# Extra identity products on TensorE in the waits of a Perceiver block

## The chip, the cores and the metric

One core of a Trainium2 chip runs the whole block in one launch. The metric is the device time of that launch in microseconds (us). The engines of the core run their own instruction streams and meet at semaphores: TensorE (matmul and transposition, PE in the profile, its weight loads PEld), VectorE (DVE), ScalarE (ACT), GpSimd (POOL) and SyncE (SP), which issues most of the DMAs.

## The reference, cut to what matters

Three residual steps on 512 latent tokens of 512 numbers (batch 8 times 64), in float32:

```
x = x + cross_attention(layernorm(x), ctx)   # 16 heads of 32, ctx: 8 x 1601 tokens
x = x + self_attention(layernorm(x))         # 16 heads of 64, 4 batches as WQ, WK, WV_down, WV_up
x = x + mixture(layernorm(x))                # 8 experts of width 2048, the best 2 for each token
```

In the reference, cross attention is a softmax over the 1601 context tokens of each batch entry and a projection. Self-attention uses only the diagonal of the softmax of the scores: the values are multiplied by the probability of the token with itself and go through WV_up, and the heads are averaged. The mixture computes gates by a softmax over 8 logits, keeps the two largest, and sums the two experts' outputs by them.

## The kernel before

Float32 products are made of three products of rounded halves: `hi` is the value rounded to the fp32r type and `lo` the rest, and hi times hi, hi times lo and lo times hi are summed (`three`, L155 to L157). ScalarE makes the hi half, VectorE or GpSimd the lo half. Data is transposed on TensorE, by a matmul with the 128x128 identity `ident` in transposing mode, and comes back through one of eight PSUM banks. Where a product is taken on plain float32 (the identity selections `new_outputs`, the gathering of tokens in gating), one call gives two weight loads and two matmul records in the trace.

**Prologue.** GpSimd makes `ident`. TensorE waits for it and then for the first context tiles (`raw_in0`), turns them (L729), and multiplies with the split weights `Wkv` as these arrive, one quarter k at a time (L752).

**Cross attention.** The loop over seven batch entries and two chunks of the context interleaves, by hand, scores, transposes of the probabilities and output products with the next chunk's keys and values. The last unit (entry 7, chunk 1) has no next chunk: step i does `turn_probs(i)` (L810), `scores(i+1)` (L799), `beside(i)` and `outputs(i)` (L822). The outputs wait for the lo half of the turned probabilities `PT` from VectorE (L635, L639). `tensor_beside` puts the output selection of the last batch entry and the first parts of the projection between these. Bank 6 holds the result of the first selection until ScalarE has copied it (`o7_in`).

**Seam.** `tensor_seam` finishes the projection (L1204 to L1206) into banks 6, 1, 3 and 0. VectorE adds and normalizes in two parts, tokens of tiles 0 to 2 (`ln_done` 2) and tile 3 (`ln_done` 3). TensorE turns both parts (L1251, L1256) and waits for their lo halves (`x2_lo`). When `ln_done` reaches 2, GpSimd also starts the lo half of the second head weights (L1276).

**Self-attention.** `tensor_heads` has a ring of banks: `take(use)` waits until the bank's former use is done. `turn_values(1)` turns the second half of the scaled values `vd` (L1507). The product with WV_up for tile 3 of the first half follows, then all four tiles of the second half (L1519 to L1521).

**Gating.** `tensor_experts` turns the normalized tokens (L2060, L2065), makes the logits, turns them (L2078), ranks the chosen experts by counting matmuls (L2086, L2089), gathers the first tile of sorted tokens by a product with a one-hot `sel` (L2103) and goes on to the loop over the experts' tiles, whose first product is L2115. VectorE runs the chain of small operations between these. After its chain it splits two 1 MB weight units (L1657) ahead of the lo half of the gathered tokens (`gT_lo`, L1961). The first layer waits for that.

**Experts.** The loop runs over tiles of 128 sorted tokens, each with eight weight units of 1 MB streamed through a ring of four buffers. It ends with a scatter back to tokens and the store.

Of the kernel before, what the change touches and what calls it, by code (L numbers as in the profile page):

```python
# [24 lines left out]
def perceiver_kernel(nc, x_in, ctx_in, Wq, bq, Wkv, bkv, Wproj, bproj,  # L25
# [3 lines left out]
    P = 128  # L29
# [34 lines left out]
    with ExitStack() as whole:  # L64
        sems = {}

        def sem(name):
            if name not in sems:
                sems[name] = whole.enter_context(nc.semaphore(name))
            return sems[name]  # L70
# [30 lines left out]
        ident = sb(0, "ident", [P, P])  # L101
# [59 lines left out]


# [149 lines left out]
        def program(block):  # L312
# [380 lines left out]
            def _(pe):  # L693
# [29 lines left out]
                pe.wait_ge(sem("ident_ready"), 2)  # L723
                pe.wait_ge(sem("raw_in0"), 16)
# [495 lines left out]
        def tensor_beside(pe, i):  # L1220
            if i == 0:
                pe.wait_ge(sem("f_turned"), 1)
                pe.wait_ge(sem("sel_ready"), 8)
                pe.wait_ge(sem("o_summed"), PAIRS_0 + NP + 1)
                new_outputs(pe, 0, slice(0, KC)).then_inc(sem("o7_turned"), 1)
            elif i == 7:
                pe.wait_ge(sem("o_summed"), PAIRS_1 + NP - 1)
                new_outputs(pe, 1, slice(0, KC - 1))
            elif i == 8:
                pe.wait_ge(sem("o7_in"), 1)  # L1230
                pe.wait_ge(sem("wp_lo"), 1)
                for t in FIRST_TILES:
                    project(pe, t, (0,))

        def tensor_seam(pe):
# [11 lines left out]
            project(pe, TT - 1, range(KC))  # L1247
            pe.wait_ge(sem("ln_done"), 2)
            for k in range(KC):
                for t in FIRST_TILES:  # L1250
                    ins = nc.tensor.matmul(bank(X_BANKS[k])[:, t * P:(t + 1) * P], xn2[:, t, k * P:(k + 1) * P],  # L1251
                                           ident[:, :], is_transpose=True, start=True, stop=True)
                ins.then_inc(sem("x2_turned"), 1)
            pe.wait_ge(sem("ln_done"), 3)
# [200 lines left out]
        def tensor_heads(pe):  # L1455
# [46 lines left out]
            def turn_values(half):  # L1502
                pe.wait_ge(sem("b_done"), USE_V[half] + TT)
# [546 lines left out]
        def tensor_experts(pe):  # L2050
# [5 lines left out]

            pe.wait_ge(sem("ln_done"), 4)
# [17 lines left out]
            ins.then_inc(sem("logits_made"), 1)  # L2075
            pe.wait_ge(sem("logits_kept"), 1)
# [4 lines left out]

            pe.wait_ge(sem("c_ready"), 5)
# [16 lines left out]

            pe.wait_ge(sem("selected"), 1)  # L2100
# [4 lines left out]
            ins.then_inc(sem("g_turned"), 1)  # L2105
            pe.wait_ge(sem("table_ready"), 1)
# [101 lines left out]
```

## Time and profile before

| | |
|---|---|
| Median of 3 runs | 1390.05 us (1389.51 to 1390.58) |
| Profiled execution, its own time | 1388.39 us |
| Span of its trace | 1386.6 us |
| Instructions | 22067 |
| TensorE busy | 1324.3 us, 96% |
| VectorE busy | 934.5 us, 67% |
| ScalarE busy | 763.1 us, 55% |
| Mean granted TensorE clock | 0.987 |

The span runs from the first to the last instruction; some 1.8 us of the execution's own time lie outside. Busy time of TensorE is the time covered by matmul records, whose ends are modelled and include the way out of the array, so in a dense stream the records overlap and their start-to-start distance is the price of one. [...]

### The profile page before, as it was taken

The numbers are of one execution on the slowest core, as the hardware profiler recorded it, in microseconds if no ns is written. First come the engines' busy times: TensorE is split into PE (matmuls) and PEld (weight loads), VectorE is DVE, ScalarE is ACT, GpSimd is POOL, SyncE is SP. The second block draws the span as 40 slices with busy tenths as digits, with TensorE's granted clock in tenths as the row PEclk, the third lists the DMA queues.
The fourth block names the chain that finished last, engine by engine and source line by source line (L and its number), as shares of the span: only waits on it lengthen the run. The fifth ranks groups of instructions, "written<-read, shape, count | busy, mean of one in ns | idle before, by whom it ended". The sixth has DMA issues, their size and how long they took to land.

```text
span 1386.6 us, 22067 instructions
## 1 busy us (share of the span) xinstructions
PE 1324.3 (96%) x7439; PEld 1149.6 (83%) x7440; DVE 934.5 (67%) x1508; ACT 763.1 (55%) x1331; POOL 106.2 (8%) x85
## 2 busy tenths in 40 slices
PE   7999999999999999999999999987899789999998
PEld 6898988888889898898889989975688578888876
DVE  5566665666667666666666766758498856388885
ACT  6465555565555555555556655554332526478872
POOL 2000000000000000000000000044443130000002
PEclk9999999999999999999999999999899889999999
DMA  5211111111111112101111011373538465399993
GB/s 197 98 52 32 32 54 40 27 45 37 43 26 42 30 34 61 30 27 45 45 34 45 23 35 29 71 142 86 91 95 304 159 223 195 127 346 355 358 355 114
DMA packets 126852, 145.11 MB, mean 105 GB/s; under 512 B 64072, under 2 KB 67528, under 8 KB 126800
## 3 DMA queue, kind: packets, MB, share of 16 engines
q1 hardware_dynamic: 125536, 140.44, 32.8%
q0 software_dynamic: 1280, 4.20, 0.9%
q8 instruction: 22, 0.36, 0.1%
q14 instruction: 14, 0.11, 0.0%
HBM read 124.75 MB, written 19.86 MB: 104 GB/s over the span
## 4 chain that ended last, share of the span: by engine, by line
PE 78%; DVE 11%; issue 5%; ACT 3%; DMA 2%; SPq 1%; DVEq 0%; POOL 0%; ACTq 0%
PE ps_scores L155 13%; PE ps_scores L157 13%; PE ps_scores L156 12%; PE ps_out L822 6%; PE ps_turn L810 5%; PE ps_scores L799 5%; PE ps_out L2141 2%; PE ps_out L2143 2%; PE ps_out L2142 2%; PE ps_turn L701 2%; PE ps_scores L2120 2%; PE ps_scores L2118 2%; PE ps_scores L2119 2%; DVE stat L626 2%; DVE Ks L551 1%
## 5 line engine op out<-in xcount | busy, mean ns | idle before, releaser
L551 DVE SCALAR_TENSOR_TENSOR Ks<-ps_scores,bkc,Ks 64x384 fp32r<-64x384 f32 (+2 forms) x254 | 160.5, 632 | 143.5 <-ACT Ks L425 140.7
L155 PE MATMUL ps_scores<-cT_hi,Wkv_hi 128*128 128x384 f32 (+2 forms) x504 | 181.9, 361 | 0.0
L513 ACT ACTIVATE Pr<-ps_scores,stat 128x705 f32<-128x705 f32 (+1 forms) x128 | 119.6, 935 | 110.1 <-DVE stat L626 110.1
L157 PE MATMUL ps_scores<-cT_hi,Wkv_lo 128*128 128x384 f32 (+2 forms) x504 | 172.9, 343 | 0.0
L156 PE MATMUL ps_scores<-cT_lo,Wkv_hi 128*128 128x384 f32 (+2 forms) x504 | 172.4, 342 | 0.0
L425 ACT ACTIVATE Ks<-ps_scores,bkc 64x384 fp32r<-64x384 f32 (+2 forms) x254 | 149.6, 589 | 39.0 <-PE ps_scores L157 35.4
L557 DVE TENSOR_TENSOR Vs<-ps_scores,Vs 128x512 fp32r<-128x512 f32 (+1 forms) x103 | 71.2, 691 | 147.7 <-ACT Vs L429 147.0
L155 PE MATMUL ps_scores<-Wkv_hi,cT_hi 128*128 128x512 f32 (+1 forms) x412 | 169.9, 412 | 0.0
L500 ACT CAST PT<-ps_turn 128x512 fp32r<-128x512 f32 (+2 forms) x256 | 110.2, 483 | 100.9 <-PE ps_turn L810 100.0
L157 PE MATMUL ps_scores<-Wkv_hi,cT_lo 128*128 128x512 f32 (+1 forms) x412 | 161.7, 393 | 0.0
L156 PE MATMUL ps_scores<-Wkv_lo,cT_hi 128*128 128x512 f32 (+1 forms) x412 | 161.1, 391 | 0.0
L2009 DVE TENSOR_TENSOR wu_lo<-wu_raw,wu_hi 128x2048 fp32r<-128x2048 f32 x56 | 126.6, 2287 | 21.2 <-ACT wu_hi L1827 21.2
L822 PE MATMUL ps_out<-PT,Vs 128*128 128x256 f32 x832 | 122.6, 285 | 18.2 <-DVE PT L639 13.9
L822 PEld LDWEIGHTS ps_out<-PT,Vs 128*128 128x128 f32 x832 | 113.0, 188 | 29.8 <-DVE PT L639 17.7
L635 DVE TENSOR_TENSOR PT<-ps_turn,PT 128x512 fp32r<-128x512 f32 (+2 forms) x256 | 130.0, 549 | 11.1 <-ACT PT L500 10.2
L429 ACT CAST Vs<-ps_scores 128x512 fp32r<-128x512 f32 (+1 forms) x103 | 60.4, 586 | 133.5 <-PE ps_scores L157 132.7
L626 DVE TENSOR_REDUCE stat<-ps_scores 128x1 f32<-128x705 f32 (+1 forms) x128 | 125.7, 983 | 3.5 <-DVE stats L677 3.4
L810 PE MATMUL ps_turn<-ident,Pr 128*128 128x128 f32 x832 | 111.6, 272 | 0.0
L1827 ACT CAST wu_hi<-wu_raw 128x2048 fp32r<-128x2048 f32 x56 | 105.4, 1915 | 5.4 <-DMA wu_raw<-in_L_ffn_W_dram 5.0
L810 PEld LDWEIGHTS ps_turn<-ident,Pr 128*128 128x128 f32 x832 | 97.6, 140 | 5.8
L157 PEld LDWEIGHTS ps_scores<-cT_hi,Wkv_lo 128*128 128x128 f32 x504 | 94.7, 188 | 5.2
L156 PEld LDWEIGHTS ps_scores<-cT_lo,Wkv_hi 128*128 128x128 f32 x504 | 95.1, 189 | 4.0
(384 smaller groups left out, 2472.4 us busy)
## 6 DMA issues: line engine op xcount, KB each, us to landing
wu_raw<-in_L_ffn_W_dram SPq DMA_DIRECT2D x64, 1024.0 KB, 7.4
raw<-in_ctx_dram SPq DMA_DIRECT2D x16, 768.0 KB, 4.5
raw<-in_ctx_dram SPq DMA_DIRECT2D x8, 1024.0 KB, 5.4
raw<-in_ctx_dram SPq DMA_DIRECT2D x8, 512.0 KB
sorted_x<-zeros SPq DMA_DIRECT2D x1, 4096.0 KB, 14.4
sorted_out<-zeros SPq DMA_DIRECT2D x1, 4096.0 KB, 25.0
o_heads<-U SPq DMA_DIRECT2D x56, 64.0 KB, 1.7
oA<-o_heads SPq DMA_DIRECT2D x8, 448.0 KB, 9.3
```

Source lines behind the costliest of these rows:

```text
L155: nc.tensor.matmul(out_ap, sh, mh, start=(i == 0), stop=False)
L156: nc.tensor.matmul(out_ap, sh, ml, start=False, stop=False)
L157: last = nc.tensor.matmul(out_ap, sl, mh, start=False, stop=(i == len(pairs) - 1))
L425: ins = nc.scalar.activation(Ks[c][0:64, 2 * i + h, o:o + wide], acc[64 * h:64 * h + 64, 0:wide], ACT.Identity, bias=bkc[:, 2 * i + h:2 * ...
L500: ins = nc.scalar.copy(PT[:, full[0]:full[-1] + 1, 0, :], acc[:, 0:P * len(full)].rearrange("p (t r) -> p t r", r=P))
L513: nc.scalar.activation(Pr[:, i % 2, 0:VALID[c]], S_cols(c, 0, VALID[c], 0 if ctx else i % 2), ACT.Exp, bias=stat[:, 0, c, i:i + 1], accum_ ...
L551: ins = nc.vector.scalar_tensor_tensor(out=Ks[c][64:128, j, o:o + wide], in0=acc[64 * h:64 * h + 64, 0:wide], scalar=bkc[:, j:j + 1], in1= ...
L626: nc.vector.tensor_reduce(stat[:, 0, c, i:i + 1], S_cols(c, 0, VALID[c], 0 if ctx else i % 2), AX.X, ALU.max, negate=True).then_inc(sem("s ...
L635: ins = nc.vector.tensor_tensor(PT[:, full[0]:full[-1] + 1, 1, :], acc[:, 0:P * len(full)].rearrange("p (t r) -> p t r", r=P), f32(PT[:, f ...
L810: ins = nc.tensor.matmul(bank(P_BANKS[q])[0:M, at:at + P], Pr[:, (i - 1) % 2, t * P:t * P + M], ident[:, :], is_transpose=True, start=True ...
L822: ins = nc.tensor.matmul(psO_heads, Vs[c][0:M, t, i - 1, :], PT[0:M, t, :, :].rearrange("p a r -> p (a r)"), start=(t == 0), stop=(t == CH ...
L2009: nc.vector.tensor_tensor(wu_lo[v][:, :, :], wu_raw[v % RING][:, :, :], f32(wu_hi[v][:, :, :]), ALU.subtract).then_inc(sem("wu_lo_done"), 1)
```

## The change

A helper `keep_busy(n, b)` makes n plain float32 products of the identity with itself, 128 columns each, into the first 128 columns of bank b. Their results are never read. It is called in 13 places, for 67 products in one execution: before the waits of the prologue (9), in steps 2 and 3 (3 each), 4 to 6 (1 each) and 7 (1 and 6) of the last unit, twice in the seam (4 and 8), once before the last turns of self-attention (6), and in gating before the turns (7), after the logits (2), after their turns (7), after the ranks (6) and after the gathering (2). Three waits come with them: in steps 2 and 3 for `o7_in`, before the 6 of self-attention for the bank's former use (`take`), and before the 7 in gating for the last uses of the banks. Nothing else changes.

```diff
--- before.py
+++ after.py
@@ -159,6 +159,11 @@
 
 
 
+
+        def keep_busy(n, b):
+
+            for _ in range(n):
+                nc.tensor.matmul(bank(b)[:, 0:P], ident[:, :], ident[:, :], start=True, stop=True)
 
         P_BANKS = (4, 5)
         C_BANK = 6
@@ -721,6 +726,7 @@
                     ins.then_inc(sem("kv_made"), 1)
 
                 pe.wait_ge(sem("ident_ready"), 2)
+                keep_busy(9, 7)
                 pe.wait_ge(sem("raw_in0"), 16)
                 for k in range(KC):
                     if k >= 3:
@@ -1223,9 +1229,16 @@
                 pe.wait_ge(sem("sel_ready"), 8)
                 pe.wait_ge(sem("o_summed"), PAIRS_0 + NP + 1)
                 new_outputs(pe, 0, slice(0, KC)).then_inc(sem("o7_turned"), 1)
+            elif i in (2, 3):
+                pe.wait_ge(sem("o7_in"), 1)
+                keep_busy(3, 6)
+            elif 4 <= i < 7:
+                keep_busy(1, 6)
             elif i == 7:
+                keep_busy(1, 6)
                 pe.wait_ge(sem("o_summed"), PAIRS_1 + NP - 1)
                 new_outputs(pe, 1, slice(0, KC - 1))
+                keep_busy(6, 6)
             elif i == 8:
                 pe.wait_ge(sem("o7_in"), 1)
                 pe.wait_ge(sem("wp_lo"), 1)
@@ -1245,12 +1258,14 @@
                 project(pe, t, range(1, KC))
             pe.wait_ge(sem("oT_lo"), KC + 1)
             project(pe, TT - 1, range(KC))
+            keep_busy(4, SPREAD_BANK)
             pe.wait_ge(sem("ln_done"), 2)
             for k in range(KC):
                 for t in FIRST_TILES:
                     ins = nc.tensor.matmul(bank(X_BANKS[k])[:, t * P:(t + 1) * P], xn2[:, t, k * P:(k + 1) * P],
                                            ident[:, :], is_transpose=True, start=True, stop=True)
                 ins.then_inc(sem("x2_turned"), 1)
+            keep_busy(8, SPREAD_BANK)
             pe.wait_ge(sem("ln_done"), 3)
             for k in range(KC):
                 ins = nc.tensor.matmul(bank(k)[:, LAST], xn2[:, TT - 1, k * P:(k + 1) * P],
@@ -1500,6 +1515,9 @@
                                 ins.then_inc(sem("b_made"), 1)
 
             def turn_values(half):
+                if half == 1:
+                    take(USE_T[1])
+                    keep_busy(6, 4 + USE_T[1] % 4)
                 pe.wait_ge(sem("b_done"), USE_V[half] + TT)
                 for j in range(HP):
                     b_out = take(USE_T[half] + j)
@@ -2054,6 +2072,8 @@
                 return nc.tensor.matmul(bank(4)[0:NE, cols], Wg_hi[:, k, :], x3T_lo[:, k, cols], start=False,
                                         stop=(k == KC - 1))
 
+            pe.wait_ge(sem("b_done"), USE_T[1] + HP)
+            keep_busy(7, X_BANKS[0])
             pe.wait_ge(sem("ln_done"), 4)
             for k in range(KC):
                 for t in FIRST_TILES:
@@ -2073,12 +2093,14 @@
             for k in range(KC):
                 ins = logits(LAST, k)
             ins.then_inc(sem("logits_made"), 1)
+            keep_busy(2, 7)
             pe.wait_ge(sem("logits_kept"), 1)
             for t in range(TT):
                 ins = nc.tensor.matmul(bank(5)[:, t * NE:(t + 1) * NE], lgT[:, t * P:(t + 1) * P],
                                        ident[0:NE, 0:NE], is_transpose=True, start=True, stop=True)
             ins.then_inc(sem("logits_turned"), 1)
 
+            keep_busy(7, 7)
             pe.wait_ge(sem("c_ready"), 5)
             pe.wait_ge(sem("chosen_ready"), 1)
             for t in range(TT):
@@ -2097,12 +2119,14 @@
                                            ident[:, :], is_transpose=True, start=True, stop=True)
                 ins.then_inc(sem("g_turned"), 1)
 
+            keep_busy(6, 7)
             pe.wait_ge(sem("selected"), 1)
             for k in range(KC):
                 for t in range(TT):
                     ins = nc.tensor.matmul(bank(6)[:, k * P:(k + 1) * P], xn3[:, t, k * P:(k + 1) * P],
                                            sel[:, t, :], start=(t == 0), stop=(t == TT - 1))
             ins.then_inc(sem("g_turned"), 1)
+            keep_busy(2, 7)
             pe.wait_ge(sem("table_ready"), 1)
             pe.wait_ge(sem("ones_r"), 1)
             pe.wait_ge(sem("b1rows_zeroed"), 1)
```

## Rows read from the trace of the kernel before

**Rows 1.** The page, part 4: engines' shares of the chain that ended last.
```profile
PE 78%; DVE 11%; issue 5%; ACT 3%; DMA 2%; SPq 1%; DVEq 0%; POOL 0%; ACTq 0%
```

**Rows 2.** Stretches of the span: busy us and count by engine, TensorE clock, DMA.
```profile
924.00:968.00 44.00, 31.31 (x186) 25.76 (x185) 33.12 (x64) 23.33 (x50) 20.85 (x14) 1.00 0.55 128
...
972.00:985.50 13.50, 8.86 (x28) 6.81 (x27) 9.35 (x16) 6.56 (x9) 8.58 (x2) 0.50 0.82 132
...
1077.80:1081.00 3.20, 3.07 (x15) 3.07 (x16) 3.20 (x4) 1.38 (x3) 2.92 (x7) 0.50 0.82 261
...
1108.50:1118.50 10.00, 5.77 (x38) 5.72 (x39) 8.93 (x28) 3.11 (x3) 5.38 (x3) 0.50 0.45 134
...
1125.00:1375.00 250.00, 248.55 (x1172) 202.24 (x1171) 169.68 (x122) 160.52 (x153) 8.18 (x9) 1.00 0.77 269
```

**Rows 3.** Timeline of TensorE, last unit: start us, us, line, out<-in [idle before <-releaser].
```profile
931.63 0.98 PE L822 MATMUL ps_out<-PT,Vs 128*128 128x256 f32 x6 [2.61 <-DVE PT L639]
932.45 0.82 PE L810 MATMUL ps_turn<-ident,Pr 128*128 128x128 f32 x6
933.02 0.57 PE L799 MATMUL ps_scores<-Ks,Qs_hi 128*128 128x354 f32 x2
...
934.85 0.98 PE L822 MATMUL ps_out<-PT,Vs 128*128 128x256 f32 x6 [0.93 <-DVE PT L639]
...
952.67 0.98 PE L822 MATMUL ps_out<-PT,Vs 128*128 128x256 f32 x6 [3.21 <-DVE PT L639]
...
959.15 1.00 PE L1215 MATMUL ps_scores<-U,sel 128*128 128x64 f32 x8
959.96 0.48 PE L1204 MATMUL ps_turn<-Wp_hi,oT_hi 128*128 128x512 f32 x1
```

**Rows 4.** Timeline of TensorE, the seam.
```profile
971.46 1.90 PE L1251 MATMUL ps_turn<-ident,xn 128*128 128x128 f32 x9 [2.08 <-DVE xn L142]
...
977.24 1.12 PE L1256 MATMUL ps_scores<-ident,xn 128*128 128x128 f32 x4 [3.24 <-DVE xn L142]
...
979.75 0.79 PE L155 MATMUL ps_turn<-x2T_hi,sW_hi 128*128 128x512 f32 x1 [1.40 <-DVE x2T_lo L1186]
```

**Rows 5.** Timeline of VectorE and GpSimd, the seam.
```profile
971.49 4.51 POOL L1276 TENSOR_TENSOR sW_lo<-sW_raw,sW_hi 128x2048 fp32r<-128x2048 f32 x1 [10.66 <-DVE xn L142]
...
973.61 2.42 DVE L132 TENSOR_TENSOR rs<-rt 128x1 f32<-128x1 f32 x1
```

**Rows 6.** Timeline of TensorE, the last turns of self-attention and the product after them.
```profile
1077.93 2.82 PE L1507 MATMUL ps_turn<-ident,vd 128*128 128x128 f32 x12 [2.68 <-DVE vd L1389]
...
1081.15 0.47 PE L1519 MATMUL ps_scores<-sW_hi,vT_hi 128*128 128x512 f32 x1
```

**Rows 7.** Timeline of VectorE before those turns.
```profile
1075.39 1.89 DVE L1389 TENSOR_TENSOR vd<-ps_turn,attn 128x512 f32<-128x512 f32 x3
```

**Rows 8.** Timeline of TensorE, gating.
```profile
1098.45 2.18 PE L2060 MATMUL ps_turn<-ident,xn 128*128 128x128 f32 x9 [3.15 <-DVE xn L142]
...
1109.88 0.17 PE L2086 MATMUL ps_turn<-chosen,before 128*128 128x8 bf16 x1 [2.90 <-DVE chosen L1930]
...
1113.24 6.37 PE L2103 MATMUL ps_turn<-sel,xn 128*128 128x128 f32 x32 [2.85 <-DVE sel L1950]
...
1121.19 0.50 PE L2115 MATMUL ps_scores<-b1rows,ones_r 128*128 128x512 f32 x1 [1.58 <-DVE gT_lo L1961]
```

**Rows 9.** Timeline of ScalarE and VectorE, gating.
```profile
1100.03 0.48 ACT L1793 CAST x3T_hi<-ps_turn 128x384 fp32r<-128x384 f32 x1 [0.16 <-PE ps_turn L2060]
...
1113.90 4.49 DVE L1657 TENSOR_TENSOR wu_lo<-wu_raw,wu_hi 128x2048 fp32r<-128x2048 f32 x2
...
1120.27 0.69 DVE L1961 TENSOR_TENSOR gT_lo<-ps_turn,gT_hi 128x512 fp32r<-128x512 f32 x1 [1.88 <-ACT gT_hi L1814]
```

**Rows 10.** Timeline of TensorE and ScalarE, prologue.
```profile
6.34 3.35 PE L729 MATMUL ps_turn<-ident,raw 128*128 128x128 f32 x16 [6.34 <-DMA raw<-in_ctx_dram]
...
11.69 0.62 ACT L442 CAST Wkv_hi<-Wkv_raw 128x512 fp32r<-128x512 f32 x1 [0.51 <-DMA Wkv_raw<-in_L_xattn_Wkv_dram]
```

## The prediction

> **What bounds the kernel now.** I read the shares of the chain that ended last first: TensorE holds 78% of it, VectorE 11% [rows 1]. Then the stretches. In the expert loop TensorE is busy 248.55 of 250 us at full clock [rows 2]. The reader is to see there that whatever is gained ahead of this loop is kept: weight transfers are issued by buffers that come free, so they move with the work. Nearly all of the kernel gives nothing to a change that only fills waits. [...] So the change is worth what the low clock costs on the path, where the extra products can prevent it, less what they delay.
>
> **Price of an extra product.** No row has the identity with itself. The nearest are plain float32 products, two records for each call. At full clock eight records with 64 columns took from 959.15 to 959.96, 0.10 us each, so a call is at least 0.20 [rows 3]. With 128 columns, 32 records took 6.37 us, nearly all of it at the low clock, 0.20 each, so a call is at most 0.40 to 0.43 there [rows 2, 8]. I take 0.21 at full clock, half of the latter, and 0.43 at the low one. A third bound: if weight loads didn't overlap, 25.76 us over 185 loads, 0.14 each, would come on top, for some 0.49 [rows 2].
>
> **The prologue.** Nine products are 3.9 us at the low clock, and TensorE waits 6.34 us for its data, so they cost nothing [rows 10]. Sixteen turns took 3.35 us, 0.20 each; at the full clock they would take 0.10. But the path goes over the last quarter of the weights: ScalarE waited 0.51 us for its DMA and began it at 11.69, long after the turns [rows 10]. The DMA is late next, whatever TensorE does. **0** (at most 0.4, the share of the first four turns).
>
> **The last unit.** Six turns took 932.45 to 933.02, 0.095 each, at full clock [rows 3]. The waits ahead of the outputs are 2.61 in step 2, 0.93 in step 3 and 3.21 in step 7 [rows 3]. Three products are 0.64, one and six are 1.5: all fit, step 3 with 0.29 to spare. The queue behind them holds only outputs that VectorE's `PT` releases. `o7_in` is up long before step 2, since the copy needs only the first selection. In this trace the clock is at 1.00 here, so I count **0**. But the waits of 2.61 and 3.21 us are as long as those after which the clock fell elsewhere, so other executions may lose here what this one did not. I price that below.
>
> **The seam.** Four products (0.86) fit the 2.08 us, eight (1.7) the 3.24, and even at the low clock eight end 0.2 late at worst (3.4 against 3.24) [rows 4]. The turns at 971.46 would be faster, nine in about 1.0 instead of 1.90. This is not worth anything: a tiny operation of VectorE took 2.42 us from 973.61, to the end of GpSimd's weight split, which ran 971.49 to 976.00 [rows 5]. GpSimd is started by `ln_done`, not by TensorE, and VectorE resumes with it. The product of L155 therefore stays at 979.75. It ran at the low clock until about 985.5, 5.75 us, and would save up to 2.9 if the clock held [rows 2, 4]. Here I chose against the gain: after the eight products end (about 974.5) there remain 2.7 us of wait, four turns of 0.4 and 2.05 more of wait. That is 4.8 us with hardly any work, more than any wait after which the clock fell. **0**, with 2.9 as the other end.
>
> **Self-attention.** `take` holds the six until VectorE's first `vd` at about 1076.05 (three took 1.89 from 1075.39) [rows 7]. They end at 1077.35, before 1077.93 [rows 6]. The added wait has nothing behind it but the turns, which wait longer. What stays is about 1.0 and 0.6 us of wait, and the clock holds. Twelve turns took 2.82 us, 0.22 each, and all sixteen 3.22 (1077.93 to 1081.15) [rows 6]. At the 0.095 to 0.10 of [rows 3] they take 1.6. Behind them is tile 3 of the first half, twelve products that wait for nothing new, so VectorE's `vT_lo` has time. What the turns gain is passed on whole: **1.6**.
>
> **Gating.** Before the turns seven products (1.5) fit the 3.15 us [rows 8]. Nine turns took 2.18, 0.24 each; at full clock the second ScalarE copy, which began at 1100.03 after waiting for TensorE, comes 0.5 earlier [rows 8, 9]. The square root of the last tile is queued behind it, so **0.5** is gained on VectorE's chain (0 to 1.2). After the logits' turns seven products (1.5) fit 2.90, after the ranks six (1.3) fit 2.85, and the last two (0.43) fit 1.58 [rows 8]. No wait above some 1.6 us is left. The gathering took 6.37 us and would take 32 times 0.107, 3.4, and the copy out would be ready 2.9 earlier [rows 8]. But VectorE is not: it splits two weight units from 1113.90 to 1118.39, which it needs no word of TensorE for, and `gT_lo`, which began at 1120.27, can begin at 1118.4 [rows 9]. So **1.9**, and VectorE is the new wait; the first product of L2115 comes at 1119.3 instead of 1121.19.
>
> [...]
>
> **The sum**, against the profiled execution's own 1388.39: 1.6 + 0.5 + 1.9 = 4.0, so 1384.4. That execution is 1.66 below the median of the runs. I can't see why in the trace, but the last unit is a candidate: one fall after its 2.61 or 3.21 us would slow the turns and outputs of a round or two by about as much as the sixteen turns lost, 1.6. The change would take that too. Against the median the gain is then 4.0 to 5.7, which gives 1384.4 to 1386.1. I forecast **1385.0**.
>
> **The rivals.**
> *The clock does not hold (0.14).* Identity products may be too thin among the waits, or not weigh as others do. For it: no row shows them. Against it: turns, which have the identity as one operand, ran from 1077.93 at 0.50 and the product right behind them at 1081.15 took 0.47, so the clock rose on turns alone [rows 2, 6]. Then each call costs 0.43. In self-attention six end at 1078.6 instead of 1077.93, 0.7 late, and the seam adds 0.2: 1390.05 + 0.9 = 1391.0, with none of the gain; 1390 if they fit.
> *It holds in one of the two places (0.08).* Either 1.6 or 2.4 comes: 1387.9 to 1388.5 against the median, some 1387.8.
> *It holds through the seam as well (0.11).* 2.9 more at most, of which a part: 1382.4.
> *Turns don't run faster (0.02).* Only the 1.9 of the gathering: 1388.1.
> *Slower (0.03).* The weight loads are not hidden, as both operands are one tile, and the clock is low: a call is 2 times (0.25 + 0.21), 0.92 (6.81 us over 27 loads from 972 [rows 2]). Then six take 5.5 us against 1.9 in self-attention (+3.6), eight 7.4 against 3.24 in the seam (+4.1), seven, seven and six in gating 6.4, 6.4 and 5.5 against 3.15, 2.90 and 2.85 (+9.5), nine 8.3 against 6.34 in the prologue (+1.9): with nothing gained, some 1409. It decides from about 0.5 a call: at 0.55 self-attention, the seam and gating add 1.4, 1.2 and 2.1. Against it: the eight records of 0.10 each had a fresh load each [rows 3].
>
> **How the numbers follow.** The forecast has 0.62. Its own range is 1383.2 to 1386.8: the 0 to 0.5 of the first turns, VectorE's part of the gathering, and the one fall more or less. Runs of this kernel spread by about 0.5 us, and about 0.2% (2.8 us) is what a measurement can tell from no change, so faster is below 1387.3 and slower above 1392.8. Faster: 0.62 of the forecast, 0.11 of the seam, 0.04 of the single place and 0.01 of the turns, 0.78 in all. Slower 0.03, within 0.2% the other 0.19. The range is 1382.2 to 1388.8: it leaves out the 0.14 of the clock that doesn't hold and the 0.03 of slower, and about 0.03 below.
>
> **What would show it.** Right: the clock at 1.00 from 1076 to the end of the gathering; `turn_values(1)` in 1.6 us; the gathering in 3.4 to 3.6 us with `gT_lo` starting right behind the second weight split, with no wait for ScalarE; the product of L155 in the seam where it was, still at 0.50 for 3 to 6 us; the loop unchanged. Wrong: extra products of over 0.3 us each; waits whose releaser has become TensorE's own queue, outputs of step 3 above all; a low clock in gating in spite of them; or the operation of 2.42 us in the seam gone, which would let the first turns count there.

## The result: 4 to 6 us less, about what was forecast

The changed kernel took 1386.18 us in the median (1383.95 to 1388.78, 11 runs) against 1390.58 (1387.79 to 1393.45, 11 runs) for the kernel before on the same chip: ratio 0.9967 [0.9957, 0.9977], by which it is 4.6 us less (3.2 to 6.0). A second comparison gave 1384.03 against 1390.05, ratio 0.9960 [0.9948, 0.9972]. The forecast was 1385.0.

The page of the changed kernel, its parts 1, 2 and 4:

```profile
span 1386.3 us, 22334 instructions
...
PE 1336.6 (96%) x7573; PEld 1162.2 (84%) x7574; DVE 935.0 (67%) x1508; ACT 762.3 (55%) x1331; POOL 105.1 (8%) x85
...
PEclk9999999999999999999999999999999999999999
...
PE 73%; DVE 13%; issue 5%; DMA 4%; ACT 3%; SPq 1%; DVEq 0%; POOL 0%; ACTq 0%
```

The span, 1386.3, is hardly below the 1386.6 of before, and DMA has 4% of the chain in place of 2% [rows 1]. So these two executions side by side don't show the gain. One has to look at each stage. Stretches of the changed kernel (columns as in [rows 2]; the clock is the mean of the granted one, 1.00 being full speed):

```profile
924.00:968.00 44.00, 35.63 (x210) 30.98 (x208) 31.86 (x62) 22.87 (x50) 18.84 (x14) 0.92 0.55 128
972.00:985.50 13.50, 8.44 (x44) 6.89 (x43) 11.31 (x19) 6.11 (x8) 7.14 (x2) 0.75 0.92 155
1077.80:1081.00 3.20, 3.01 (x27) 2.82 (x27) 3.20 (x4) 1.21 (x3) 1.89 (x3) 1.00 1.06 363
1106.00:1116.00 10.00, 7.44 (x74) 7.09 (x74) 8.71 (x34) 4.67 (x4) 4.14 (x2) 1.00 0.37 133
1125.00:1375.00 250.00, 246.45 (x1159) 200.08 (x1158) 167.21 (x119) 160.10 (x152) 8.19 (x9) 1.00 0.76 267
```

The clock is at 1.00 in self-attention and gating, where it was 0.50 [rows 2]. It is still low in a part of the seam (0.75 from 972 to 985.5, 0.50 from 980 on). In the last unit it is 0.92, where before had 1.00. TensorE's timeline of the changed kernel (columns as in [rows 3]; L166 is `keep_busy`, two records a call):

```profile
938.38 0.98 PE L828 MATMUL ps_out<-PT,Vs 128*128 128x256 f32 x6 [0.70 <-DVE PT L644]
...
940.51 0.38 PE L166 MATMUL ps_turn<-ident 128*128 128x128 f32 x2
943.19 0.98 PE L828 MATMUL ps_out<-PT,Vs 128*128 128x256 f32 x6 [2.30 <-DVE PT L644]
...
947.18 1.65 PE L828 MATMUL ps_out<-PT,Vs 128*128 128x256 f32 x6 [0.71 <-DVE PT L644]
...
971.17 1.05 PE L166 MATMUL ps_scores<-ident 128*128 128x128 f32 x8
973.41 1.20 PE L1265 MATMUL ps_turn<-ident,xn 128*128 128x128 f32 x9 [1.18 <-DVE xn L142]
...
974.77 1.95 PE L166 MATMUL ps_scores<-ident 128*128 128x128 f32 x16
979.20 1.12 PE L1271 MATMUL ps_scores<-ident,xn 128*128 128x128 f32 x4 [2.47 <-DVE xn L142]
981.71 0.79 PE L155 MATMUL ps_turn<-x2T_hi,sW_hi 128*128 128x512 f32 x1 [1.40 <-DVE x2T_lo L1192]
...
1077.31 1.60 PE L166 MATMUL ps_turn<-ident 128*128 128x128 f32 x12 [0.88 <-DVE vd L1404]
1079.10 1.53 PE L1525 MATMUL ps_turn<-ident,vd 128*128 128x128 f32 x12 [0.19 <-DVE vd L1404]
...
1080.82 0.47 PE L1537 MATMUL ps_scores<-sW_hi,vT_hi 128*128 128x512 f32 x1
...
1098.12 1.20 PE L2080 MATMUL ps_turn<-ident,xn 128*128 128x128 f32 x9 [1.59 <-DVE xn L142]
...
1112.29 3.84 PE L2126 MATMUL ps_turn<-sel,xn 128*128 128x128 f32 x32 [1.41 <-DVE sel L1968]
...
1118.27 0.49 PE L2139 MATMUL ps_scores<-b1rows,ones_r 128*128 128x512 f32 x1 [1.70 <-DVE gT_lo L1979]
```

Sixteen turns of self-attention go from 1079.10 to 1080.82, 1.72 us instead of 3.22 [rows 6]. The gathering takes 3.84 instead of 6.37, and from its start to the first expert product there are 5.98 us instead of 7.95 [rows 8]. The outputs of 947.18, at a clock of 0.50, take 1.65 where others take 0.98. VectorE at the gathering of the changed kernel:

```profile
1112.95 4.49 DVE L1675 TENSOR_TENSOR wu_lo<-wu_raw,wu_hi 128x2048 fp32r<-128x2048 f32 x2
1117.35 0.68 DVE L1979 TENSOR_TENSOR gT_lo<-ps_turn,gT_hi 128x512 fp32r<-128x512 f32 x1
```

`gT_lo` stands right behind the second weight split and waits for nothing, where it waited 1.88 us for ScalarE [rows 9]. VectorE is the bound there now.

**The expert loop's share.** The loop began at 1118.27, 2.9 us earlier than before, and took 268.0 us instead of 265.4. ScalarE's group of the high parts of the weights, on the page of three kernels (busy, mean ns | idle before, releaser), shows where this comes from. The changed kernel:

```profile
L1845 ACT CAST wu_hi<-wu_raw 128x2048 fp32r<-128x2048 f32 x56 | 105.5, 1916 | 10.8 <-DMA wu_raw<-in_L_ffn_W_dram 10.5
```

The kernel before, profiled a second time:

```profile
L1827 ACT CAST wu_hi<-wu_raw 128x2048 fp32r<-128x2048 f32 x56 | 105.2, 1916 | 6.5 <-DMA wu_raw<-in_L_ffn_W_dram 6.4
```

The fastest version below:

```profile
L1847 ACT CAST wu_hi<-wu_raw 128x2048 fp32r<-128x2048 f32 x56 | 105.0, 1916 | 2.1 <-DMA wu_raw<-in_L_ffn_W_dram 1.9
```

Waits for the weights of 10.5, 6.4 and 1.9 us go with loops of 268.0, 265.8 and 263.9. On the pages of all fourteen traces below these waits (1.9 to 10.5) and the length of the loop have a correlation of 0.95. Whether the longer loop is the change's doing or chance is the first thing for the experiments.

### The profile page after: what moved, and what is told of

The parts are those of the page before. It is cut to its first block, busy times and chain, and to the rows that moved or that the text cites. A ratio compares the mean times of both kernels' runs of the same rounds, so it can differ in the third digit from the quotient of the medians.

```text
span 1386.3 us, 22334 instructions
## 1 busy us (share of the span) xinstructions
PE 1336.6 (96%) x7573; PEld 1162.2 (84%) x7574; DVE 935.0 (67%) x1508; ACT 762.3 (55%) x1331; POOL 105.1 (8%) x85
## 3 DMA queue, kind: packets, MB, share of 16 engines
q1 hardware_dynamic: 125536, 140.44, 32.8%
## 4 chain that ended last, share of the span: by engine, by line
PE 73%; DVE 13%; issue 5%; DMA 4%; ACT 3%; SPq 1%; DVEq 0%; POOL 0%; ACTq 0%
PE ps_scores L155 13%; PE ps_scores L157 13%; PE ps_scores L156 12%; PE ps_out L828 6%; PE ps_turn L816 5%; PE ps_scores L805 5%; DMA wu_raw<-in_L_ffn_W_dram 3%; PE ps_turn L706 2%; PE ps_out L2165 2%; PE ps_out L2167 2%; PE ps_out L2166 2%; DVE stat L631 2%; PE ps_scores L2144 2%; PE ps_scores L2142 2%; PE ps_scores L2143 2%
## 5 line engine op out<-in xcount | busy, mean ns | idle before, releaser
L155 PE MATMUL ps_scores<-cT_hi,Wkv_hi 128*128 128x384 f32 (+2 forms) x504 | 181.9, 361 | 0.0
L155 PE MATMUL ps_scores<-Wkv_hi,cT_hi 128*128 128x512 f32 (+1 forms) x412 | 169.9, 412 | 0.0
L828 PE MATMUL ps_out<-PT,Vs 128*128 128x256 f32 x832 | 123.2, 286 | 13.8 <-DVE PT L644 9.5
L828 PEld LDWEIGHTS ps_out<-PT,Vs 128*128 128x128 f32 x832 | 113.5, 189 | 24.9 <-DVE PT L644 12.9
L1845 ACT CAST wu_hi<-wu_raw 128x2048 fp32r<-128x2048 f32 x56 | 105.5, 1916 | 10.8 <-DMA wu_raw<-in_L_ffn_W_dram 10.5
L816 PEld LDWEIGHTS ps_turn<-ident,Pr 128*128 128x128 f32 x832 | 98.2, 141 | 5.7
```

Source lines behind the costliest of these rows:

```text
L155: nc.tensor.matmul(out_ap, sh, mh, start=(i == 0), stop=False)
L816: ins = nc.tensor.matmul(bank(P_BANKS[q])[0:M, at:at + P], Pr[:, (i - 1) % 2, t * P:t * P + M], ident[:, :], is_transpose=True, start=True ...
L828: ins = nc.tensor.matmul(psO_heads, Vs[c][0:M, t, i - 1, :], PT[0:M, t, :, :].rearrange("p a r -> p (a r)"), start=(t == 0), stop=(t == CH ...
```

## The experiments

Theory: the extra products cost nothing where they fit a wait, hold the clock, and are worth what the low clock cost right behind them. Rivals: the loop gives the lead back; the gain comes from another place than I said; any instruction, not streamed columns, would do.

In all of them I read the same edges off TensorE's timeline, which makes one table. **Unit**: first outputs after 926 us (L828) to the first product with `spread`. **Seam**: from there to the first L155. **To turns**: from there to the last sixteen turns of self-attention. **Turns**: to the product behind them. **Gating**: first turns on `xn` to the gathering. **Gathering**: its start to the first expert product. Then the start and the length of the loop, to the end of the span. From the turns to gating it was 17.3 us in every trace. All in us.

| kernel | unit | seam | to turns | turns | gating | gathering | loop start | loop |
|---|---|---|---|---|---|---|---|---|
| before | 30.7 | 22.3 | 98.2 | 3.22 | 14.8 | 7.95 | 1121.2 | 265.4 |
| e9, before again | 32.8 | 22.3 | 97.3 | 1.72 | 14.8 | 8.16 | 1121.2 | 265.8 |
| changed | 32.6 | 22.4 | 97.4 | 1.72 | 14.2 | 5.98 | 1118.3 | 268.0 |
| e8, changed again | 31.0 | 22.3 | 98.3 | 1.72 | 14.2 | 5.99 | 1117.5 | 265.6 |
| e1, gating alone | 31.0 | 22.3 | 98.0 | 3.11 | 14.2 | 6.00 | 1118.7 | 264.4 |
| e2, self-attention alone | 31.9 | 22.3 | 98.2 | 1.72 | 16.4 | 7.94 | 1122.6 | 267.4 |
| e3, last unit alone | 32.1 | 22.3 | 97.0 | 1.72 | 14.8 | 7.98 | 1120.2 | 264.9 |
| e4, seam, prologue alone | 31.9 | 22.2 | 97.2 | 1.72 | 16.2 | 7.61 | 1121.0 | 267.0 |
| e7, 8 columns | 31.9 | 22.3 | 97.4 | 1.72 | 16.2 | 7.56 | 1121.0 | 267.6 |
| e10, without self-attention | 31.1 | 22.2 | 98.4 | 3.33 | 14.2 | 5.99 | 1119.5 | 263.9 |
| e5, seam filled | 30.8 | 22.3 | 95.6 | 1.72 | 14.1 | 5.99 | 1114.6 | 267.6 |
| e6, seam and unit filled | 32.1 | 22.2 | 95.6 | 1.72 | 14.2 | 5.98 | 1116.0 | 263.9 |
| e12, the same again | 31.7 | 22.3 | 95.6 | 1.72 | 14.1 | 5.99 | 1115.7 | 265.4 |
| e11, step 7 filled too | 30.4 | 22.3 | 95.6 | 1.72 | 14.2 | 5.99 | 1114.3 | 267.4 |

### One part at a time

**Gating alone** (the kernel before with these; the other parts left out):

```diff
+            pe.wait_ge(sem("b_done"), USE_T[1] + HP)
+            keep_busy(7, X_BANKS[0])
             pe.wait_ge(sem("ln_done"), 4)
...
+            keep_busy(2, 7)
             pe.wait_ge(sem("logits_kept"), 1)
...
+            keep_busy(7, 7)
             pe.wait_ge(sem("c_ready"), 5)
...
+            keep_busy(6, 7)
             pe.wait_ge(sem("selected"), 1)
```

> Only the 24 extra products of gating (7, 2, 7, 6 and 2) are left. My sum: the first turns of gating come 0.5 us earlier and the gathering takes 3.4 to 3.7 us instead of 6.4, of which VectorE's two weight splits let 1.9 through, so 2.4 us less than before (ratio 0.9983) and the clock at 1.00 from the turns to the first expert product. A rival: the expert loop gives back what comes before it, since in the changed kernel its ten tiles took 2.6 us longer with waits for weight transfers; then the ratio is 0.9995 or more although the loop starts 2.4 us earlier against the end of self-attention.

1387.57 against 1390.58 (the four of this set share the runs of before), ratio 0.9983 [0.9969, 0.9997], 2.4 us less. The clock was at 1.00 in all of gating. It is the only part whose gain stands clear in the time and in the table: gating 14.2 and gathering 6.00, in every trace that has these products, against 14.8 to 16.4 and 7.6 to 8.2 in the others.

**Self-attention alone:**

```diff
             def turn_values(half):
+                if half == 1:
+                    take(USE_T[1])
+                    keep_busy(6, 4 + USE_T[1] % 4)
                 pe.wait_ge(sem("b_done"), USE_V[half] + TT)
```

> Only the 6 extra products before the last turns of self-attention are left. My sum: the sixteen turns take 1.6 to 1.7 us instead of 3.2 where the clock had fallen, so 1.6 us in executions like the profiled one, and about 1.0 on the mean if the clock falls only in some of them (ratio 0.9988 to 0.9993). If the gain of the places adds up, it is what is left of 4.4 us after gating and the last unit. If the clock fell there rarely, the ratio is 1.000.

1391.52, ratio 1.0001 [0.9988, 1.0013]: nothing. The sixteen turns do take 1.72. But its gating took 16.4, 1.6 more than before's, so in this trace the gain was lost again. Stretches of this kernel, the turns and then the first part of gating:

```profile
1077.80:1081.00 3.20, 3.01 (x28) 2.82 (x27) 3.20 (x4) 1.10 (x3) 1.79 (x3) 1.00 1.07 385
1098.00:1105.50 7.50, 5.82 (x26) 3.47 (x27) 6.63 (x16) 2.30 (x6) 0.00 (x0) 0.60 0.00 0
```

Here the low clock fell on the products of the logits as well (0.60 on the mean, against 1.00 from 1097.5 to 1105.5 in the changed kernel). e4 and e7 have that too and before and e3 don't, so it isn't the six products that bring it.

**The last unit alone** (16 products, steps 2 to 7):

```diff
+            elif i in (2, 3):
+                pe.wait_ge(sem("o7_in"), 1)
+                keep_busy(3, 6)
+            elif 4 <= i < 7:
+                keep_busy(1, 6)
             elif i == 7:
+                keep_busy(1, 6)
                 pe.wait_ge(sem("o_summed"), PAIRS_1 + NP - 1)
                 new_outputs(pe, 1, slice(0, KC - 1))
+                keep_busy(6, 6)
```

> Only the 16 extra products of the last unit are left. My prediction counted 0 from the trace and up to 1.6 for a fall that other executions may have: ratio 0.9988 to 1.000. The rival is that the two new waits and the products delay outputs: step 3 had 0.29 us to spare and shows 0.25 of wait in the changed kernel, so no more than 0.1 us is lost; a ratio above 1.0005 would speak for it.

1388.01, ratio 0.9984 [0.9972, 0.9996]. By the time alone this is a gain of 2.2, but its trace has no such gain. The unit took 32.1, and its clock was:

```profile
924.00:968.00 44.00, 36.03 (x212) 31.73 (x211) 31.88 (x62) 23.19 (x50) 20.92 (x14) 0.92 0.55 129
```

That is no better than without. But by its mean clock (0.988) the profiled execution is the worst of the twelve, the others have 0.989 to 0.991. What all twelve say stands behind e9 below; with the error found there the gain is probable, not shown.

This trace has a cost that I didn't expect. In step 3 the clock was low (0.50 from 935.2 to 936.3), the three products took 1.49 us instead of 0.83, and they outlasted the wait:

```profile
935.18 1.49 PE L166 MATMUL ps_turn<-ident 128*128 128x128 f32 x6
935.24 0.28 DVE L644 TENSOR_TENSOR PT<-ps_turn,PT 65x128 fp32r<-65x128 f32 x1
936.32 1.14 PE L827 MATMUL ps_out<-PT,Vs 128*128 128x256 f32 x6
```

`PT` was done at 935.52, and the outputs began at 936.32 behind the products. In step 2 of the same trace they began 0.05 us after it, so 0.75 us were lost.

**Seam and prologue alone** (nine products ahead of the first turns, four and eight in the seam, everything else left out):

```diff
+                keep_busy(9, 7)
                 pe.wait_ge(sem("raw_in0"), 16)
...
+            keep_busy(4, SPREAD_BANK)
             pe.wait_ge(sem("ln_done"), 2)
...
+            keep_busy(8, SPREAD_BANK)
             pe.wait_ge(sem("ln_done"), 3)
```

> Only the 9 extra products of the prologue and the 4 and 8 of the seam are left. My prediction counts 0 for both: the prologue waits for the last quarter of the weights, and in the seam VectorE stands until GpSimd's split ends and the clock falls all the same in the wait behind the eight. Ratio 0.9997 to 1.0003, and the first product of self-attention at a granted clock of 0.50. The rival is that the seam's products hold the clock or let it rise earlier in many executions: up to 2.9 us, a ratio down to 0.998.

1389.18, ratio 0.9992 [0.9978, 1.0006]: nothing that can be measured. The way to the turns is 97.2 to 98.4 in the four traces with the 4 and 8 products, and 97.0 to 98.2 in the five without any.

### The seam, filled

The changed kernel with the two remaining waits of the seam filled as well:

```diff
-            keep_busy(8, SPREAD_BANK)
+            keep_busy(18, SPREAD_BANK)
...
+            pe.wait_ge(sem("x2_lo"), 1)
+            keep_busy(8, X_BANKS[0])
             pe.wait_ge(sem("x2_lo"), KC + 1)
```

> The changed kernel with its seam filled: 18 extra products instead of 8 behind the first turns (3.8 us of a wait of some 4.4 at full clock), and 8 new ones, after a wait for the first lo half, between the last turns and the first product of self-attention (1.7 us). My reading is that the 8 alone leave 2.5 and 1.4 us of wait with four turns between, after which the clock falls in any execution. If so, it now stays at 1.00 and the product of L155 runs at the full clock: 2 to 2.9 us less than the changed kernel, a ratio to before of 0.9947 to 0.9953. If extra products don't count as other work does, or if the fall comes from elsewhere, the first product still meets 0.50 and the ratio is that of the changed kernel, 0.9967.

1383.74, ratio 0.9961 [0.9947, 0.9975]. TensorE in the seam of this kernel:

```profile
971.64 1.20 PE L1265 MATMUL ps_turn<-ident,xn 128*128 128x128 f32 x9 [1.19 <-DVE xn L142]
...
973.01 4.18 PE L166 MATMUL ps_scores<-ident 128*128 128x128 f32 x36
977.42 0.66 PE L1271 MATMUL ps_scores<-ident,xn 128*128 128x128 f32 x4 [0.23 <-DVE xn L142]
977.92 2.02 PE L166 MATMUL ps_turn<-ident 128*128 128x128 f32 x16
979.88 0.49 PE L155 MATMUL ps_turn<-x2T_hi,sW_hi 128*128 128x512 f32 x1
```

The clock is at 1.00 from 972 to 985.5, and the first L155 takes 0.49 instead of 0.79 [rows 4], but the seam itself is still 22.3 us: the turns of 977.42 can't come earlier. What is won lies behind it, 95.6 us to the turns instead of 97.0 to 98.4. That held in all four traces that have this edit. The mean of the ten others is 97.7, so 2.1 us. Even so the ratio is that of the changed kernel, measured on the same chip (0.9960), and not the 0.9947 to 0.9953 that I expected: with intervals of 0.13% to either side 2.1 us (0.15%) is hardly to be told, and here the loop took 267.6.

### Streamed columns or any instruction

The changed kernel with extra products of 8 columns instead of 128:

```diff
-                nc.tensor.matmul(bank(b)[:, 0:P], ident[:, :], ident[:, :], start=True, stop=True)
+                nc.tensor.matmul(bank(b)[:, 0:8], ident[:, :], ident[:, 0:8], start=True, stop=True)
```

> The changed kernel with its 67 extra products cut from 128 to 8 columns, so that each still loads the 128-column identity twice but streams next to nothing. If the clock follows the streamed work, it falls in gating as before the change, and the ratio is 0.999 to 1.000 (0.0 to 1.4 us gained). If weight loads or the mere issue hold it, gating shows 1.00 and the ratio is near 0.9967. A record should take 0.10 us with 8 columns too, as those of 64 columns did, which says that the load sets the price.

1390.41, ratio 1.0009 [0.9995, 1.0023]: the gain is gone. Timeline of TensorE in gating, this kernel:

```profile
1093.97 1.62 PE L166 MATMUL ps_turn<-ident 128*128 128x8 f32 x14
1097.29 2.06 PE L2080 MATMUL ps_turn<-ident,xn 128*128 128x128 f32 x9 [1.69 <-DVE xn L142]
...
1110.45 2.10 PE L166 MATMUL ps_out<-ident 128*128 128x8 f32 x12
1113.45 5.97 PE L2126 MATMUL ps_turn<-sel,xn 128*128 128x128 f32 x32 [0.89 <-DVE sel L1968]
```

Fourteen records with 8 columns take 1.62 us; with 128 they took 1.72 (1094.81 in the changed kernel). They have as many weight loads and fill the wait nearly as long, yet the gathering takes 5.97 us, much as in the kernel before. The granted clock from 1084 to 1120 is 0.81, as in both traces of the kernel before, and 1.00 in the changed kernel. So what held the clock here is that the products stream 128 columns, not that they are issued or that they load weights. Busy time doesn't show that: from 1084 to 1120 TensorE is busy 30.55 us in this kernel and 28.20 in the changed one.

### How much is chance

The changed kernel and, in another set, the kernel before were run again as kernels of their own:

> The changed kernel once more, for a second trace and a time beside the three others. The gating keeps 1.00 whatever the phase, the seam falls again, the last unit may or may not fall. The loop from the first expert product to the end took 265.4 us before the change and 268.0, 264.4, 267.4, 264.9 and 267.0 in the five traces since: if its waits for weight transfers come by chance, it lies anywhere in 264 to 268 here; if the changed kernel starves it, it is again near 268.

1384.03, ratio 0.9960 [0.9948, 0.9972]; loop 265.6 this time.

> The kernel before, once more, for a second trace of it. Theory: the clock falls at places by chance that differs from execution to execution, and the first trace of it was one in which the last unit had been spared. Of the four traces so far in which the last unit has no extra products three fell in it, of the four in which self-attention has none two fell ahead of the last turns. So this trace has a fall in the last unit with a chance of 3 in 4, the seam and gating fall in any case, the seam's from about 972 and gating's ahead of the gathering, and its gathering takes 6 to 6.4 us. Rival: the falls belong to the kernel and its code, not to the execution, and the two traces of this kernel agree: 1.00 throughout the last unit and a fall ahead of the last turns of self-attention. Ratio 1.000 in both cases.

1389.08 against 1390.57, ratio 0.9992 [0.9979, 1.0004] for the same code. That is the error of such a comparison, 0.1%, and it makes the 0.9984 of e3 weak. The trace is another than the first one of this kernel. Its last unit, and its last turns:

```profile
924.00:968.00 44.00, 34.79 (x177) 29.51 (x176) 31.80 (x61) 22.71 (x50) 18.75 (x14) 0.84 0.54 128
```

```profile
1079.18 1.53 PE L1507 MATMUL ps_turn<-ident,vd 128*128 128x128 f32 x12 [2.68 <-DVE vd L1389]
1080.54 0.60 PE L1507 MATMUL ps_out<-ident,vd 128*128 128x128 f32 x4
1080.90 0.48 PE L1519 MATMUL ps_scores<-sW_hi,vT_hi 128*128 128x512 f32 x1
```

The clock was 0.84 in the unit where it had been 1.00, and the same wait of 2.68 us ahead of the turns [rows 6] had no fall behind it: 1.72 us. So whether the clock falls in a given wait differs between executions of one program.

**The clock of all runs.** A trace is one execution, but the mean granted clock is on record for each run. The time at the low clock is about 2 times (1 − clock) times the span, which is an estimate: it takes the 0.50 of the low stretches [rows 2] for every one of them, and the clock has three decimals. The means, with standard errors of 0.7 to 1.5 us:

| runs | us at the low clock |
|---|---|
| before, the 35 runs beside the four parts | 36.4 |
| gating alone | 23.6 |
| self-attention alone | 38.2 |
| last unit alone | 28.2 |
| seam and prologue alone | 31.0 |
| changed, first and second time | 12.8, 9.7 |
| 8 columns, and before beside it | 38.7, 36.1 |

By these estimates the last unit's products hold the clock in part (28.2 against 36.4), more than its single trace shows. Those of seam and prologue do too (31.0), and still the time is the same within its interval. For the six of self-attention the clocks show nothing.

**Without self-attention's six** (the changed kernel less the lines of e2):

> The changed kernel without the six products of self-attention. Theory: the clock ahead of the last turns falls in about half of the executions, at 1.6 us each, so the mean loses 0.8 us at most against the changed kernel (1386.5 or 1384.5 by the two times it has had, so a ratio of 0.9965 to 0.997), and if it falls here it is seen as sixteen turns in 3.2 us instead of 1.7. Rival: they are worth nothing at all, even where the clock would have fallen, because what the turns gain is waited for again behind them; then the trace has the turns at 3.2 us and the wait of VectorE behind them is shorter by as much. Third: worth the whole 1.6 as I predicted, ratio 0.998.

1385.4, ratio 0.9966 [0.9952, 0.9979]. The fall was there in this trace (0.51 from 1078.6 to 1082):

```profile
1078.69 2.82 PE L1522 MATMUL ps_turn<-ident,vd 128*128 128x128 f32 x12 [2.69 <-DVE vd L1404]
1081.31 0.97 PE L1522 MATMUL ps_out<-ident,vd 128*128 128x128 f32 x4
1082.02 0.49 PE L1534 MATMUL ps_scores<-sW_hi,vT_hi 128*128 128x512 f32 x1
```

Turns of 3.33 us, followed by the same 17.3 to gating as after the 1.72. So nothing behind the turns takes the gain back: the rival of this run falls. Of the six traces with no extra product there, three had the fall (before, e1, e10); of the seven with the six products of 128 columns, none had. These are few: if the products did nothing, all three falls would still land among the six about once in 14 times. Half of 1.5 us is 0.8 on the mean, which is too little for these ratios.

### Is a lead kept, and a faster version

The seam as in e5, and in steps 4, 5 and 6 of the last unit 2, 6 and 5 products:

```diff
-                keep_busy(1, 6)
+                keep_busy((2, 6, 5)[i - 4], 6)
```

> As the run before, and in the last unit 2, 6 and 5 extra products instead of 1 each in steps 4, 5 and 6, where the changed kernel's clock fell in its profiled execution after a wait of 2.30 us with one product in it. If waits of over 2 us are what costs, the clock is at 1.00 from the unit to the loop, and the ratio is another 0.0005 to 0.001 lower, 0.994 to 0.995. If the 5 and 6 outlast their waits (2.06 and 1.71 us against 1.3 and 1.1), outputs of these steps show TensorE's own queue ahead of them and the ratio rises.

1382.13 (5 runs), ratio 0.9951 [0.9936, 0.9965]. The unit wasn't shorter, 32.1. There was one fall left ahead of the loop, after a wait in step 7 (0.63 from 953.9 to 955.2; this kernel's timeline):

```profile
949.85 1.50 PE L166 MATMUL ps_turn<-ident 128*128 128x128 f32 x12
953.14 0.98 PE L828 MATMUL ps_out<-PT,Vs 128*128 128x256 f32 x6 [1.79 <-DVE PT L644]
953.96 1.21 PE L816 MATMUL ps_turn<-ident,Pr 128*128 128x128 f32 x6
```

The next kernel fills that wait too, 13 products for 6:

```diff
                 new_outputs(pe, 1, slice(0, KC - 1))
-                keep_busy(6, 6)
+                keep_busy(13, 6)
```

> The version with the seam and the last unit filled, and thirteen products instead of six after the outputs of step 7, since its only fall came behind a wait of 1.79 us there. Theory: the seven more fit that wait (7 times 0.21, 1.5), the clock is at 1.00 from the prologue to the loop's end, and the time is 0.3 to 0.8 us lower on the mean: ratio 0.9945 to 0.9955, with a start of the loop at 1114.5 to 1116. Rival: the last unit is then bound by VectorE, and holding its clock gains nothing more: ratio 0.9955 or higher, start at 1116. Slower would be: the outputs wait for products that still run, ratio above 0.996.

1386.56, ratio 0.9967 [0.9952, 0.9982]. The trace is what the theory said: a clock of 1.00 up to the last 2 us of the span, the shortest unit of all (30.4) and the earliest loop (1114.3). In part that is luck, since the wait ahead of the outputs of step 2, with the same three products in it, was 0.73 us here, 2.22 in e6 and 2.99 in e12, whose one fall came there. The time is not what the theory said: the profiled loop took 267.4, and the ratio is that of the changed kernel. I had named a ratio above 0.996 as the sign of outputs that wait for running products, but in this trace each of them waits for VectorE (0.22 to 1.66 us). That raised the question of e12, the kernel of e6 once more:

> The version with the seam and the last unit filled (18 and 8 products in the seam, 2, 6 and 5 in steps 4 to 6), once more, because it had few runs. What is to be told apart: is a start of the loop that is some 5 to 6.9 us earlier passed on whole? Theory: yes, on the mean, since the loop took 263.9 to 268.0 us in thirteen traces whatever its start, so the ratio is 0.9950 to 0.9960 again and the start of the loop 1114.5 to 1116. Rival: the last version, with the clock held everywhere and the earliest start of all (1114.33), gained no more than the changed kernel did (0.9967), so beyond a start of about 1117 the loop waits for its weights and gives the rest back: then this one too has a ratio of 0.9963 to 0.997, and its loop takes 266 us or more.

1384.24 against 1391.17, ratio 0.9957 [0.9942, 0.9972], start 1115.7, loop 265.4: within what the theory expected, outside what the rival did, though its interval reaches into the rival's range. Over the fourteen traces the loop took 263.9 to 268.0 us (1.5 standard deviation) at starts from 1114.3 to 1122.6, and the correlation of the two is 0.01. A line through the thirteen sets of runs with a measured ratio, time against start of the loop, has a slope of 0.8 (0.5 to 1.1): a microsecond won ahead of the loop is worth about one at the end. Three fit it badly: e7 and e11 are 2.6 and 2.0 us above it, e10 is 2.2 below. The intervals of the ratios, up to 0.15% to either side (2.1 us), are nearly as wide, but what it was is not settled. The version of e6 is the fastest measured, with 0.9951 and 0.9957. Its lead over the changed kernel (0.9967 and 0.9960) is of the size of the intervals, so probable, not shown.

## Why the prediction was right, and where it wasn't

**Price of a product.** I took 0.21 at full clock. Eight records (four calls) took 1.05, sixteen 1.95 and fourteen 1.72, so 0.24 to 0.26 a call with the end of the last record in it, and 36 in a row 4.18, 0.23 a call. The weight loads don't come on top: the 36 of that row took 4.10 beside the records (e5). The slower rival needed 0.5.

**Prologue, 0.** Right: the nine calls fit, and the first outputs after 926 us start within 926.7 to 927.0 in all fourteen traces.

**Last unit, 0, with up to 1.7 for falls of other executions.** The falls were seen rightly, but not that most would stay. Other executions do have them (four of the five traces of the unit without products do, 30.7 to 32.8 us, mean 31.7), and they cost time there. The unit took 30.4 to 30.8 us with a clock of 1.00 from 924 to 968 (three traces), 31.0 to 32.1 with 0.96 (five), 31.9 to 32.6 with 0.92 (five) and 32.8 with 0.84 (e9). That is some 0.6 us for a step of 0.04. The 16 products leave most of these falls (30.8 to 32.6, mean 31.5, in five traces). The step that failed: I reckoned that they would take the one fall away, and looked only at the waits of steps 2 and 7. Steps 4 to 6 have a single product each and kept waits of 2.30 us (changed) and 2.13 (e8), after which the clock fell (0.50 from 947.2 to 948.2, and 0.80 on the mean from 943 to 948). The filled steps kept enough as well: it fell behind 2.29 us in step 2 and 1.82 in step 7 (e3, 0.57 from 953.5 to 955.5), and behind 1.81 in step 7 (e10, 0.57 from 952 to 956). By the clocks of the runs of e3 the 16 products save 8 us at the low level. At 0.6 us for 3.5 of them that would be 1.4 (an estimate), so how much this part gains stays open. Step 3's wait was 0.25 where I had 0.29, at full clock. That outputs could be late there at the low clock was my own sign of being wrong, and e3 has it once, with 0.75 us.

**Seam, 0.** Right, and for the reason given: the operation of 2.42 us came again on VectorE (here the changed kernel):

```profile
975.55 2.43 DVE L132 TENSOR_TENSOR rs<-rt 128x1 f32<-128x1 f32 x1
```

The seam kept its 22.3 us, also where the clock was at 1.00 in all of it (e5, e6, e11, e12). The clock didn't hold across the wait of 2.47: 1.00 from 974.7 to 976.8 and 0.50 from 980 to 985.5. The other end, 2.9, came to 2.1 once it was filled.

**Self-attention, 1.6.** The size was right, 1.5 (3.22 to 1.72), passed on whole, with the six ending before the turns. What was wrong is that I took a fall seen in one trace for one that always comes. It comes in half of the traces: 0.8. No ratio shows that amount.

**Gating, 0.5 and 1.9.** The gathering was right to a tenth: 7.95 to 5.98, with VectorE as the new wait in the place named. The first part was mis-sized: 14.8 to 14.2 against the trace that I had, 0.6, but others without the products have 16.2 and 16.4, so 1.2 on the mean of five, the end of my 0 to 1.2.

**The sum.** From the means of the table: unit 0.1, seam −0.1, turns 0.8, gating 1.2, gathering 1.9, together 3.9 us. I had 4.0 against the profiled execution and 5.0 against the median. The two comparisons give 4.6 (3.2 to 6.0) and 5.6 (3.9 to 7.2). So the forecast of 1385.0 rests on two errors that cancel in part: too much for self-attention and, by the traces, for the unit, too little for gating. In that measure the forecast was lucky. The 0.7 to 1.7 between the stages and the comparisons lies within the intervals, and I have no row for it; part of it can be the unit's, see above. In the rival of a single place I also subtracted wrongly: 1390.05 less 2.4 is 1387.7, not 1387.9, which changes nothing else.

**Turns and the clock.** At full clock sixteen turns took 1.72 us (e9: 1.00), at the low one 3.11 to 3.33 (e1 and e10: 0.51), in the same place with the same wait. So the rival in which turns don't run faster (0.02) is out. The stretches at 0.50 that the forecast was priced from, in the seam, at the last turns and in gating [rows 2], lie behind waits of 1.40 to 3.24 us [rows 4, 6, 8]. That such a wait brings the fall every time is not shown: e9 had 2.68 us there and stayed at 1.00.

**The loop.** "Unchanged" is right on the mean only. A single trace moves by 4 us with its waits for weights, as much as the whole change.

## What to carry to other kernels

Products without a use in TensorE's waits are worth what the low clock costs right behind the wait (here 3.11 to 3.33 us instead of 1.72 for sixteen turns, 6.37 instead of 3.84 for a gathering), and only where TensorE ends that stage. Gating paid 2.4 us. The seam kept its 22.3 us even at full clock, because VectorE ends it, and the gain came behind it. In the last unit sixteen products left most of the falls (clocks of 0.92 to 1.00 in five traces). Fill a wait whole, and with wide products: 67 of 8 columns held nothing (0.81 from 1084 to 1120, where 128 columns had 1.00). Reckon also with their length at the low clock, at which three of them made outputs 0.75 us late. And read a thing that falls by chance, as the clock does (1.00 and 0.84 in the last unit of one program), from several traces of the same kernel before it gets a full price in a sum.

## What I had not expected of the hardware

- The same program, with the same wait of 2.68 us, ran the sixteen turns behind it once at 0.50 (3.22 us) and once at 1.00 (1.72 us).
- A float32 product with 8 columns takes nearly the time of one with 128 (0.116 against 0.123 us a record, 14 records each, both at a clock of 1.00) and 67 of them held the clock no better than none (0.81 from 1084 to 1120, the same as before the change).
- The loop's waits for weights vary from 1.9 to 10.5 us between executions with the same transfers, and the loop from 263.9 to 268.0.
